# A transformer decoder on one core: the rotary swap of layer 2 by transfers, and a new order of two turns

## The chip, the cores and the metric

The kernel runs on one core of one Trainium2 chip. The metric is the device time of one execution in microseconds, as a median of several runs. The engines are TensorE (PE in the rows; PEld is its weight load), VectorE (DVE), ScalarE (ACT), GpSimd (POOL) and SyncE (SP), which here only issues transfers.

## The reference

128 sequences of 64 tokens with 128 features (`x`) go through four decoder layers. Each has an attention with 16 heads of 8 features, a cross attention to `ctx_1024` and a feed-forward part, each followed by a residual sum and a layer norm. What matters here is attention:

```
q, k, v = x @ wq + bq, x @ wk + bk, x @ wv          # per token; some layers without a bias
q, k    = rope(q), rope(k)                           # layers 0 and 2, and layer 3's cross attention
p       = softmax(q @ k.T / sqrt(8) + mask)          # per sequence and head, 64 x 64
x       = layernorm(x + (p @ v) @ wo + bo)
```

A rotation is `part * cos + swapped(part) * sin`. In layer 0 and layer 3 `swapped` exchanges neighbouring features. In layer 2 it exchanges the two halves of the 128 features: feature i with feature i + 64.

## The kernel before, in words

The 8192 tokens lie in 64 tiles of 128 rows in `X`, and all stages work on pairs of tiles (256 tokens, four sequences), so on 32 pairs. `attention(...)` builds one attention stage. It gives a generator per engine (`sync`, `gpsimd`, `tensor`, `scalar`, `vector`), whose `slot(T)` issues what the engine does in step T for several pairs at once; `all_pairs` runs the steps, those in the middle as a hardware loop of two pairs. The order within an engine is the order of the code, and semaphores (`made`, `parity_wait`) tie the engines together. Two stages can be run one behind the other, with the last four steps of the first interleaved with the first steps of the second: L1x with L1f, and L2a with L2x. L0a, L0x and L3x run alone. L1f and L2x share the memory, and so the tile names, of L1x and L2a.

What one pair passes through, with the step T in which it happens (T is the pair whose scores are made in this step):

- GpSimd copies its rows to `XS` (L498) in step T - 3. TensorE turns them into the bank `psF` (`fill_turn`, L584) in step T - 2, and ScalarE copies that to `XT` (L719; in L3x a copy of 512 columns, L717).
- In the same step TensorE projects `XT` to keys (`fill_projection`, L597) in `psF`, ScalarE copies them out, and then the queries follow in the same way. With rope (L0a, L2a, L3x) a second projection with swapped weights `ks`, `qs` gives the swapped part (L599), and ScalarE copies both parts with their biases to `RK` (`raw_parts`, L703 and L704). `psF` is one bank, so turn, keys, queries and values follow each other.
- GpSimd multiplies `RK` with the table of cosines and sines (`rope_product`, L404) and adds the two halves to the keys in `KT` (L524), and likewise to the queries in `QT` (L529). This stands at the end of its step, for pair T + 2. SyncE then sends the keys to `KB` in four transfers (L385), from where the scores use them.
- TensorE makes the scores in `psS` (L569), for L2a behind a fixed mask (L563). VectorE takes the maximum (L781) and subtracts it (L784), ScalarE takes the exponential (L756). In step T + 1 TensorE turns the probabilities (`turn_probs`, L617, four groups of four), ScalarE copies them (L697), TensorE multiplies them with the values (L683), and VectorE normalises to `ON` (L848).
- In step T + 2 TensorE turns `ON` (L630) into a half of the bank that the turned probabilities use too, ScalarE copies it to `OT` (L711), TensorE projects it (L672), and VectorE adds the residual rows (L816) and takes the statistics (L825, L836). The residual rows come with the bias added by GpSimd (`XR`, L482), except in L0x (`by_rows`), where TensorE adds the bias with a matmul (L670) and VectorE adds `X` itself.
- In step T + 3 GpSimd makes the root (L459, L461) and VectorE writes the normalised rows to `X` (L805).

In a step TensorE's order is: scores, turn of `ON` (L630), turn of the new rows (L584), first group of probabilities, key projection, two groups, query projection, last group, output projection, values times probabilities, value projection (`fill_v`, L609). ScalarE copies in the order `OT`, `XT`, first group, keys, two groups, queries, last group, then the exponential and the copy of the values to `VB` (L771). L0x gets its rows another way (`fill_rows`), without `fill_turn`; GpSimd rotates them as rows there (`rope_rows`).

## Time and profile before

| | us |
|---|---|
| median of 3 runs | 4016.08 (4015.06 to 4021.43) |
| the profiled execution | 4011.83 |
| its span, first to last instruction | 4010.0 |
| TensorE busy in it | 3481.2 |
| VectorE, ScalarE, GpSimd busy | 2993.7, 2291.8, 1885.8 |

The span and the busy times are of the one profiled execution; the median is of runs without a profile. Busy times are averages over stages with different limits, so the rows below are read stage by stage. In the execution L0a makes its scores from 27 to 309 us, L0x from 351 to 590, L1x and L1f from 1568 to 2067, L2a and L2x from 2409 to 2947, L3x from 3539 to 3857. The other parts of the span (routed experts, grouped attention, a recurrent block) are not touched.

### The profile page before, as it was taken

Reading aid. Unit: us, or ns where it says so; the run is one execution under the profiler, and the core shown is the slowest. Engines: PE = TensorE matmul, PEld = TensorE weight load, DVE = VectorE, ACT = ScalarE, POOL = GpSimd, SP = SyncE. Lnnn points to the kernel's source line nnn. Section 1 sums busy time; section 2 is a strip of 40 time slices with the busy share of each in tenths; the row PEclk is TensorE's granted clock in tenths of the full one; section 3 lists DMA queues with packets and bytes.
Section 4 is the critical chain, followed back from the end, with each engine's and each line's share of the span. In section 5 each row is a group of like instructions: output and inputs, shape, how many; then the busy total and the mean of one; then the engine's idle time right before and its main releaser. Section 6 shows DMA issues by size and latency. Waiting matters only on the chain. (4 is left out here: it accounts for less than half of the span.)

```text
span 4010.0 us, 127677 instructions
## 1 busy us (share of the span) xinstructions
PE 3481.2 (87%) x46840; PEld 2654.2 (66%) x46840; DVE 2993.7 (75%) x6186; ACT 2291.8 (57%) x3920; POOL 1885.8 (47%) x2970
## 2 busy tenths in 40 slices
PE   8996996797999998999987839999989688879985
PEld 6885775465777776878875627778854254457764
DVE  6986995155898886888863477888867588659975
ACT  5775771344444444778752447777754466556653
POOL 6887864655441111224545436652223355457754
PEclk9997995899999998999986969999989799989988
DMA  2002213697000000110005820001112000000001
GB/s 82 29 27 80 69 54 103 180 262 196 19 16 3 0 0 29 50 49 19 17 19 155 240 70 16 14 25 53 49 42 65 23 0 0 1 26 27 26 8 42
DMA packets 311910, 219.08 MB, mean 55 GB/s; under 512 B 52689, under 2 KB 290257, under 8 KB 311505
## 3 DMA queue, kind: packets, MB, share of 16 engines
q1 hardware_dynamic: 251824, 166.57, 14.3%
q0 software_dynamic: 12288, 25.19, 2.0%
q10 hardware_dynamic: 47520, 23.60, 2.0%
q8 instruction: 177, 2.90, 0.3%
q14 instruction: 101, 0.82, 0.1%
HBM read 131.27 MB, written 54.53 MB: 46 GB/s over the span
## 5 line engine op out<-in xcount | busy, mean ns | idle before, releaser
L781 DVE TENSOR_REDUCE L2a_mx<-L2a_psS 128x32 f32<-128x2048 f32 x64 | 146.7, 2292 | 75.8 <-PE L2a_psS L569 75.8
L781 DVE TENSOR_REDUCE L1x_mx<-L1x_psS 128x32 f32<-128x2048 f32 x64 | 146.7, 2292 | 74.5 <-PE L1x_psS L569 74.5
L2474 POOL TENSOR_TENSOR L1a_rs<-L1a_ag,eps 128x1 f32<-128x1 f32 x64 | 13.0, 204 | 397.8 <-DVE L1a_ag L2639 397.8
L1111 POOL DMA_INDIRECT L0f_sorted_x<-X,L0f_IDX x128 | 123.0, 961 | 93.8 <-DMA L0f_sorted_x<-X,L0f_IDX 35.6
L1530 DVE TENSOR_TENSOR L0f_G<-L0f_SG,L0f_psH 128x512 f32<-128x512 f32 x106 | 73.0, 689 | 120.1 <-ACT L0f_SG L1274 72.7
L459 POOL TENSOR_TENSOR L1x_rs<-L1x_mv,eps 128x2 f32<-128x2 f32 x64 | 12.5, 195 | 310.5 <-DVE L1x_mv L836 310.5
L784 DVE TENSOR_TENSOR L2a_PR<-L2a_psS,L2a_mx 128x2048 f32<-128x2048 f32 x64 | 146.7, 2292 | 7.3
L784 DVE TENSOR_TENSOR L1x_PR<-L1x_psS,L1x_mx 128x2048 f32<-128x2048 f32 x64 | 146.7, 2292 | 7.3 <-DVE L1x_mx L781 0.2
L697 ACT ACTIVATE L2a_PT<-L2a_psP 128x512 f32<-128x512 f32 x256 | 146.0, 598 | 2.9 <-PE L2a_psP L617 1.4
L697 ACT ACTIVATE L1x_PT<-L1x_psP 128x512 f32<-128x512 f32 x256 | 145.9, 595 | 3.0 <-PE L1x_psP L617 1.4
L617 PE MATMUL L1x_psP<-W,L1x_PR 128*128 128x128 f32 x1024 | 146.9, 277 | 0.2
L617 PE MATMUL L2a_psP<-W,L2a_PR 128*128 128x128 f32 x1024 | 145.7, 276 | 0.2
L756 ACT ACTIVATE L1x_PR<-L1x_PR 128x2048 f32<-128x2048 f32 x64 | 122.3, 1912 | 37.0 <-DVE L1x_PR L784 37.0
L2563 PE MATMUL L1a_psO<-rest_WO,L1a_OT 128*64 128x128 f32 x2048 | 125.9, 276 | 11.5 <-ACT L1a_OT L2588 7.4
L756 ACT ACTIVATE L2a_PR<-L2a_PR 128x2048 f32<-128x2048 f32 x64 | 122.6, 1915 | 18.5 <-DVE L2a_PR L784 18.5
L617 PEld LDWEIGHTS L1x_psP<-W,L1x_PR 128*128 128x128 f32 x1024 | 118.0, 142 | 20.7 <-ACT L1x_PT L697 13.9
L617 PEld LDWEIGHTS L2a_psP<-W,L2a_PR 128*128 128x128 f32 x1024 | 120.0, 142 | 17.6 <-ACT L2a_PT L697 7.9
L683 PE MATMUL L1x_psB<-VB,L1x_PT 128*64 128x18 f32 x4096 | 131.4, 212 | 0.0
L2497 PE MATMUL L1a_psF<-L1a_XT,rest_WQ 128*128 128x256 f32 x512 | 131.0, 390 | 0.5 <-DVE L1a_KT L2449 0.5
L2563 PEld LDWEIGHTS L1a_psO<-rest_WO,L1a_OT 128*64 128x64 f32 x2048 | 110.5, 137 | 31.4 <-ACT L1a_OT L2588 31.3
L683 PE MATMUL L2a_psB<-VB,L2a_PT 128*64 128x18 f32 x4096 | 131.2, 212 | 0.0
L683 PEld LDWEIGHTS L1x_psB<-VB,L1x_PT 128*64 128x64 f32 x4096 | 125.0, 138 | 7.8 <-issue 0.4
(624 smaller groups left out, 11625.1 us busy)
## 6 DMA issues: line engine op xcount, KB each, us to landing
L0f_WB<-in_w12a SPq DMA_DIRECT2D x53, 312.0 KB, 3.8
L0f_XB<-L0f_sorted_x SPq DMA_DIRECT2D x53, 256.0 KB, 4.0
L0f_sorted_y<-L0f_YB ACTq DMA_DIRECT2D x53, 256.0 KB, 3.8
L1m_WB<-in_w12b SPq DMA_DIRECT2D x37, 321.0 KB, 4.1
L1m_XB<-L1m_sorted_x SPq DMA_DIRECT2D x37, 256.0 KB, 4.0
L1m_sorted_y<-L1m_YB ACTq DMA_DIRECT2D x37, 256.0 KB, 4.4
L0x_VS<-in_ctx SPq DMA_DIRECT2D x64, 128.0 KB, 2.7
KB<-L1x_QK SPq DMA_DIRECT2D x256, 32.0 KB, 1.8
```

Source lines behind the costliest of these rows:

```text
L459: nc.gpsimd.tensor_tensor(rs[:, F.u, 0, :], mv[:, F.u, :, 1], eps[:, 0:2], ALU.add).then_inc(S["var_eps"].sem, 1)
L617: m = nc.tensor.transpose(psP[:, bank, n, :], PR[:, A.u, r, b:b + 2, :].rearrange("p h k -> p (h k)"), ident)
L683: m = nc.tensor.matmul(psB[64 * s:64 * s + 64, (j * HP + b) * VW:(j * HP + b + 1) * VW], PT[:, j, b, 64 * s:64 * s + 64], VB[:, A.u, 2 * j ...
L697: nc.scalar.activation(PT[:, j, 4 * hb:4 * hb + 4, :], psP[:, bank], ACT.Copy).then_inc(S["pt_a"].sem, 1)
L756: nc.scalar.activation(PR[:, T.u], PR[:, T.u], ACT.Exp, scale=scale).then_inc(S["probs"].sem, 1)
L781: nc.vector.tensor_reduce(mx[:, T.u, :], sc, AX, ALU.max).then_inc(S["maxed"].sem, 1)
L784: nc.vector.tensor_tensor(PR[:, T.u].rearrange("p r h k -> p (r h) k"), sc, mx[:, T.u, :].unsqueeze(2).to_broadcast([P, 2 * HEADS, SEQ]), ...
L1111: nc.gpsimd.indirect_dma_start(out=sorted_x[p][:, :], out_offset=bass.IndirectOffsetOnAxis(ap=IDX[:, k, t:t + 1], axis=0), in_=X[:, t, :], ...
L1530: nc.vector.tensor_tensor(G[0:f, J % 2, c, :], SG[0:f, c, :], up, ALU.mult).then_inc(S["g_ready"].sem, 1)
L2474: nc.gpsimd.tensor_tensor(rs[:, A.par, 0:1], ag[:, A.par, 1:2], eps[:, 0:1], ALU.add).then_inc(S["var_eps"].sem, 1)
L2497: m = nc.tensor.matmul(bank[:, 256 * j:256 * j + 256], WQ[:, 2 * k + j, :], XT[:, N.u, :], start=True, stop=True)
L2563: m = nc.tensor.matmul(psJ[64 * s:64 * s + 64, :], OT[:, s, c, :], WO[:, s, c, :], start=c == 0, stop=c == QC - 1, skip_group_check=True)
```

## The change

Three things change in `attention`.

- **The swap of layer 2 (L2a, `halves=True`).** The projections with swapped weights are gone, and so are their copies. ScalarE copies only the first part of keys and queries to `RK`, and SyncE makes the second part with two transfers per pair: partitions 64 to 127 to partitions 0 to 63, and the other way round, each of both keys and queries (64 partitions of two runs of 1 KB, 128 KB). They are issued behind the four key transfers of the pair before. `RK` gets two places. GpSimd's rotation moves from the end of its step, where it was for pair T + 2, to right behind the root, for pair T + 1, and waits for the transfers; the key transfers are for pair T + 1 as well.
- **The order.** TensorE turns the new rows (L584) ahead of `ON` (L630), and ScalarE copies `XT` ahead of `OT`. This holds for all stages but L0x.
- **The bias of L0x.** It is added by GpSimd to the residual rows, as in the other stages, and TensorE's matmul with it is gone.

The row writes (L805) stay as they were. On ScalarE a `pace` (one semaphore increment) stands ahead of the copies to `RK`.

```diff
@@ -251,13 +251,14 @@
-        def attention(L, q, k, v, o, qs=None, ks=None, bq=None, bqs=None, bk=None, bks=None, bo=None,
+        def attention(L, q, k, v, o, qs=None, ks=None, bq=None, bqs=None, bk=None, bks=None, bo=None, halves=False,
                       cq=0, ck=0, cross=False, norm=None, mask=None, ln_o=False, affine=None, keep=None, tally=False, arrive=False, tables=None, follows=None):
...
             by_rows = tables is not None
-            turned = ks is not None
+            turned = ks is not None or halves
+            ahead = 1 if halves else 2
             turn_c = cross and norm is not None and not by_rows
@@ -271,7 +272,7 @@
             RA = mem.sb("RA", [P, 2, 2, 2 * P]) if by_rows else None
-            RK = mem.sb("RK", [P, 2, 512]) if turned else None
+            RK = mem.sb("RK", [P, 2, 2, 512]) if turned else None
             QK = mem.sb("QK", [P, 2, 2, 2 * P])
@@ -313,8 +314,7 @@
             srcv = (CV if raw else CT) if cross else XT
-            bias_on_pe = by_rows
-            bias_row = rowx[:, 0, :] if ln_o else None if bias_on_pe else bo
+            bias_row = rowx[:, 0, :] if ln_o else bo
@@ -376,13 +376,22 @@
                         sp.dma_start(CV[:, K.u, :], io["ctxT"][:, bass.ds(K.p * 256, 256)]).then_inc(parity_sem("side_in", K), 16)
-                    if K.ok:
-                        made(sp, "k_roped" if turned else "o_k", K.p + 1)
+                    B = T + ahead if turned else K
+                    if B.ok:
+                        made(sp, "k_roped" if turned else "o_k", B.p + 1)
                         pace(sp, S)
-                        made(sp, "scores", K.p - 1)
+                        made(sp, "scores", B.p - 1)
                         for b in range(HQ):
-                            sp.dma_start(KB[b:P:HQ, K.u, b, :, :].rearrange("p s k -> p (s k)"), KT[b:P:HQ, K.u, :]).then_inc(parity_sem("keys_in", K), 16)
+                            sp.dma_start(KB[b:P:HQ, B.u, b, :, :].rearrange("p s k -> p (s k)"), KT[b:P:HQ, B.u, :]).then_inc(parity_sem("keys_in", B), 16)
+                    if halves and K.ok:
+                        made(sp, "o_k", K.p + 1)
+                        pace(sp, S)
+                        made(sp, "o_q", K.p + 1)
+                        for n in range(2):
+                            here, there = slice(64 * n, 64 * n + 64), slice(64 - 64 * n, 128 - 64 * n)
+                            sp.dma_start(RK[here, K.u, :, 256:512], RK[there, K.u, :, 0:256]).then_inc(parity_sem("stored", K), 16)
                     if mask is by_key and K.ok:
@@ -398,9 +407,13 @@
-            def rope_product(eng, n, tab):
-                parts = RK[:, n].rearrange("p (c s k) -> p c s k", c=2, s=4)
+            def kept(M):
+                return M.u if halves else 0
+            def rope_product(eng, M, n, tab):
+                parts = RK[:, kept(M), n].rearrange("p (c s k) -> p c s k", c=2, s=4)
                 return eng.tensor_tensor(parts, parts, rope[:, tab:tab + 2, :].unsqueeze(2).to_broadcast([P, 2, 4, SEQ]), ALU.mult)
@@ -442,6 +455,27 @@
+                def rotate(M):
+                    if turned and M.ok:
+                        if not products_on_dve:
+                            if halves:
+                                parity_wait(g, "stored", M, 32)
+                            else:
+                                made(g, "o_k", M.p + 1)
+                            rope_product(nc.gpsimd, M, 0, ck).then_inc(S["gates"].sem, 1)
+                        made(g, "gates", M.p + 1)
+                        parity_wait(g, "keys_in", M - 2, 16 * HQ)
+                        nc.gpsimd.tensor_tensor(KT[:, M.u], RK[:, kept(M), 0, 0:256], RK[:, kept(M), 0, 256:512], ALU.add).then_inc(S["k_roped"].sem, 1)
+                        if halves:
+                            parity_wait(g, "stored", M, 32)
+                        else:
+                            made(g, "o_q", M.p + 1)
+                        rope_product(nc.gpsimd, M, 1, cq).then_inc(S["gates_out"].sem, 1)
+                        made(g, "gates_out", M.p + 1)
+                        made(g, "scores", M.p - 1)
+                        nc.gpsimd.tensor_tensor(QT[:, M.u], RK[:, kept(M), 1, 0:256], RK[:, kept(M), 1, 256:512], ALU.add).then_inc(S["q_roped"].sem, 1)
@@ -465,6 +499,8 @@
                             nc.gpsimd.tensor_tensor(rows_of(F), RB[:, F.u], rs[:, F.u, 1, :].unsqueeze(2).to_broadcast([P, 2, D]), ALU.mult).then_inc(S["out_rows"].sem, 1)
+                    if halves:
+                        rotate(T + 1)
                     A = T - 2
@@ -513,20 +549,8 @@
                         mean_squares(N.p, CS[:, N.u], 0, MC[:, N.u, :], "stat_root", "means")
-                    M = T + 2
-                    if turned and M.ok:
...
+                    if not halves:
+                        rotate(T + 2)
                     Y = T - 4
@@ -622,6 +646,9 @@
                     yield
+                    if N.ok and not by_rows:
+                        fill_turn(N)
+                    yield
                     if H.ok:
@@ -629,9 +656,6 @@
                         m.then_inc(S["o_turned"].sem, 1)
-                    yield
-                    if N.ok and not by_rows:
-                        fill_turn(N)
                     yield
@@ -666,10 +690,8 @@
                             made(pe, "res", H.p)
-                        if bias_on_pe:
-                            nc.tensor.matmul(psJ, ident, bo.unsqueeze(1).to_broadcast([P, 2, D]), start=True, stop=False, skip_group_check=True)
                         for a in range(2):
-                            m = nc.tensor.matmul(psJ[:, a, :], OT[:, H.u, a * P:a * P + P], o, start=not bias_on_pe, stop=True, skip_group_check=bias_on_pe)
+                            m = nc.tensor.matmul(psJ[:, a, :], OT[:, H.u, a * P:a * P + P], o, start=True, stop=True)
                         m.then_inc(S["proj"].sem, 1)
@@ -696,20 +718,17 @@
-                def raw_parts(n, biases):
+                def raw_parts(N, n, biases):
+                    if halves:
+                        return nc.scalar.activation(RK[:, N.u, n, 0:256], psF[:, 0:256], ACT.Identity, bias=biases[0])
                     if biases[0] is None:
-                        return nc.scalar.activation(RK[:, n, :], psF[:, :], ACT.Copy)
-                    nc.scalar.activation(RK[:, n, 0:256], psF[:, 0:256], ACT.Identity, bias=biases[0])
-                    return nc.scalar.activation(RK[:, n, 256:512], psF[:, 256:512], ACT.Identity, bias=biases[1])
+                        return nc.scalar.activation(RK[:, 0, n, :], psF[:, :], ACT.Copy)
+                    nc.scalar.activation(RK[:, 0, n, 0:256], psF[:, 0:256], ACT.Identity, bias=biases[0])
+                    return nc.scalar.activation(RK[:, 0, n, 256:512], psF[:, 256:512], ACT.Identity, bias=biases[1])
...
                     A, N, H = T - 1, T + 2, T - 2 - e
-                    if H.ok:
-                        made(act, "o_turned", H.p + 1)
-                        made(act, "proj", H.p - 1)
-                        nc.scalar.activation(OT[:, H.u, :], flat(psOT), ACT.Copy).then_inc(S["ot"].sem, 1)
-                    yield
                     if N.ok and not by_rows:
@@ -717,6 +736,11 @@
                             nc.scalar.activation(XT[:, N.u, :], psF[:, 0:256], ACT.Copy).then_inc(S["o_tx"].sem, 1)
+                    yield
+                    if H.ok:
+                        made(act, "o_turned", H.p + 1)
+                        made(act, "proj", H.p - 1)
+                        nc.scalar.activation(OT[:, H.u, :], flat(psOT), ACT.Copy).then_inc(S["ot"].sem, 1)
                     yield
@@ -729,8 +753,9 @@
                         elif turned:
-                            made(act, "k_roped", N.p)
-                            raw_parts(0, (bk, bks)).then_inc(S["o_k"].sem, 1)
+                            made(act, "k_roped", N.p - 1 if halves else N.p)
+                            pace(act, S)
+                            raw_parts(N, 0, (bk, bks)).then_inc(S["o_k"].sem, 1)
                         else:
@@ -742,8 +767,9 @@
                         if turned:
-                            made(act, "q_roped", N.p)
-                            raw_parts(1, (bq, bqs)).then_inc(S["o_q"].sem, 1)
+                            made(act, "q_roped", N.p - 1 if halves else N.p)
+                            pace(act, S)
+                            raw_parts(N, 1, (bq, bqs)).then_inc(S["o_q"].sem, 1)
                         else:
...
@@ -2670,8 +2697,8 @@
-        turning = attention("L2a", Wm("L2q"), Wm("L2k"), Wm("L2v"), Wm("L2o"), qs=Wm("L2qs"), ks=Wm("L2ks"), bq=C("L2bq"), bqs=C("L2bqs"),
-                  bk=C("L2bk"), bks=C("L2bks"), bo=rowb[:, 2, :], cq=2, ck=2, mask=static)
+        turning = attention("L2a", Wm("L2q"), Wm("L2k"), Wm("L2v"), Wm("L2o"), halves=True, bq=C("L2bq"), 
+                  bk=C("L2bk"), bo=rowb[:, 2, :], cq=2, ck=2, mask=static)
         run(turning, attention("L2x", Wm("L2xq"), Wm("L2xk"), Wm("L2xv"), Wm("L2xo"), bq=C("L2xbq"), bk=C("L2xbk"), bo=rowb[:, 3, :], cross=True, follows=turning))
```

## Rows read from the trace of the kernel before

**Rows 1.** Line L781, one stretch per stage: duration ns; first to last start, us.

```profile
L781 DVE TENSOR_REDUCE L0x_mx<-L0x_psS x27: 2280/2291/2292, 368.9 to 567.8; 128x32 f32<-128x2048 f32 x27
...
L781 DVE TENSOR_REDUCE L1x_mx<-L1x_psS x26: 2291/2292/2292, 1601.0 to 1802.1; 128x32 f32<-128x2048 f32 x26
...
L781 DVE TENSOR_REDUCE L2a_mx<-L2a_psS x27: 2291/2292/2293, 2446.6 to 2687.9; 128x32 f32<-128x2048 f32 x27
...
L781 DVE TENSOR_REDUCE L2a_mx<-L2a_psS x28: 2291/2292/2293, 2720.1 to 2931.7; 128x32 f32<-128x2048 f32 x28
...
L781 DVE TENSOR_REDUCE L3x_mx<-L3x_psS x27: 2280/2292/2294, 3571.5 to 3838.4; 128x32 f32<-128x2048 f32 x27
```

**Rows 2.** Stretches: us; busy us (count) of PE, PEld, DVE, ACT, POOL; clock; DMA.

```profile
100.00:190.00 90.00, 88.17 (x1596) 73.73 (x1596) 81.60 (x140) 63.73 (x111) 76.60 (x161) 1.00 0.09 29
430.00:540.00 110.00, 98.91 (x1749) 83.69 (x1747) 106.85 (x156) 82.39 (x130) 96.89 (x172) 1.00 0.23 69
2480.00:2640.00 160.00, 154.44 (x2779) 127.49 (x2777) 140.41 (x191) 118.54 (x222) 102.16 (x138) 1.00 0.04 14
3620.00:3800.00 180.00, 170.90 (x2605) 133.58 (x2603) 169.33 (x318) 123.79 (x226) 133.65 (x212) 1.00 0.08 26
```

**Rows 3.** Timeline, TensorE, a pair of L2a: start, length in us, instruction [idle].

```profile
2548.38 0.44 PE L630 MATMUL L2a_psP<-W,L2a_ON 128*128 128x128 f32 x2
2548.66 0.38 PE L584 MATMUL L2a_psF<-W,L2a_XS 128*128 128x128 f32 x2
2548.88 0.60 PE L617 MATMUL L2a_psP<-W,L2a_PR 128*128 128x128 f32 x4
2549.65 0.70 PE L597 MATMUL L2a_psF<-L2a_XT,W 128*128 128x256 f32 x2 [0.17 <-ACT L2a_XT L719]
2550.18 0.59 PE L599 MATMUL L2a_psF<-L2a_XT,W 128*128 128x256 f32 x2
2550.61 1.04 PE L617 MATMUL L2a_psP<-W,L2a_PR 128*128 128x128 f32 x8
2551.79 0.48 PE L597 MATMUL L2a_psF<-L2a_XT,W 128*128 128x256 f32 x1
...
2556.35 0.64 PE L563 MATMUL L2a_psS<-causal,pick 32*64 32x512 bf16 x16
```

**Rows 4.** Timeline of GpSimd and SyncE in the same pair of L2a.

```profile
2551.81 1.28 POOL L404 TENSOR_TENSOR L2a_RK<-L2a_RK,rope 128x512 f32<-128x512 f32 x1 [2.33 <-ACT L2a_RK L704]
2553.17 0.73 POOL L524 TENSOR_TENSOR L2a_QK<-L2a_RK 128x256 f32<-128x256 f32 x1
...
2554.06 2.39 SPq L385 DMA_DIRECT2D KB<-L2a_QK  x4
```

**Rows 5.** Transfers of the run: count, KB each, us from issue to landing.

```profile
L0x_VS<-in_ctx SPq DMA_DIRECT2D x64, 128.0 KB, 2.7
...
KB<-L2a_QK SPq DMA_DIRECT2D x256, 32.0 KB, 1.8
...
L2a_CR<-in_ctxT SPq DMA_DIRECT2D x32, 128.0 KB, 2.1
```

**Rows 6.** Groups by line, L2a, last L2x: count | busy us, mean ns.

```profile
L805 DVE TENSOR_SCALAR X<-L2a_RB,L2a_mv,L2a_rs 128x128 f32 x29 | 30.0, 1072 | 0.0
...
L482 POOL TENSOR_TENSOR L2a_XR<-X,rowb 128x256 f32<-128x256 f32 x14 | 10.4, 743 | 0.0
...
L805 DVE TENSOR_SCALAR X<-L2a_RB,L2a_mv,L2a_rs 128x128 f32 x26 | 7.7, 340 | 0.0
```

**Rows 7.** Timeline of ScalarE and TensorE at a step's start in L2x.

```profile
2813.16 0.78 ACT L771 ACTIVATE VB<-L2a_psF 64x256 f32<-64x256 f32 x2
...
2814.10 0.44 PE L630 MATMUL L2a_psP<-W,L2a_ON 128*128 128x128 f32 x2
```

**Rows 8.** Waits of TensorE, 120 us of L3x: us in total, times, longest.

```profile
PE L3x_psF L597 <- ACT L3x_CX L717: 3.5, 12, 0.3
```

**Rows 9.** Waits of GpSimd in 90 us of L0x.

```profile
POOL L0x_rs L459 <- DVE L0x_mv L836: 10.3, 12, 0.9
```

14 lines of the change are left out of this document (2 added, 12 removed).

## The prediction

> **What bounds the kernel now.** The change touches seven attention stages that have one loop body. Each handles 32 pairs of tiles, so the first thing to read is the time per pair. [rows 1] gives it, as the distance from the first to the last reduction of a stretch over the number of steps between them. L0x takes (567.8 - 368.9) / 26 = 7.65 us, L1x 201.1 / 25 = 8.04, L2a 241.3 / 26 = 9.28, L2x 211.6 / 27 = 7.84 and L3x 266.9 / 26 = 10.27. L0a is not shown; L1f, which follows L1x as L2x follows L2a, has the work of L2x.
>
> Next come the busy times of such stretches [rows 2]. In L2a TensorE is busy for 154.4 of 160 us and VectorE for 140.4, so TensorE is the bound. In L0x VectorE is busy for 106.9 of 110, TensorE for 98.9 and GpSimd for 96.9: VectorE is the bound, with GpSimd not far behind. L0a (TensorE 88.2 of 90) and L3x (170.9 of 180) are bound by TensorE too, though in L3x VectorE (169.3) is almost level. TensorE's granted clock is 1.00 in all four, the 2.4 GHz level; with TensorE as full as this after the change I see no reason for it to fall.
>
> Then one pair of L2a on TensorE [rows 3]. Matmuls overlap, so a group's cost is the time from its start to the next group's start; where nothing is waited for, that is its modelled length less 0.17 (L597: 0.70 long, L599 starts 0.53 later). A swapped twin, L599, costs 0.43 (2550.18 to 2550.61), and there are two of them per pair. The four transposes at 2548.88 should cost 0.60 - 0.17 = 0.43, but the key projection starts 0.77 after them: TensorE stands for 0.33 us until ScalarE has copied XT. The eight at 2550.61 should cost 0.87, but the query projection starts 1.18 after them: it stands for 0.3 us, now because ScalarE must copy the keys and their swapped twin out of the bank first. These two stalls and the two twins are what the change reaches.
>
> **L2a, part by part.** The swapped halves of keys and queries no longer come from a second projection, so two L599 groups of 0.43 go: -0.86 per pair. The key copy on ScalarE is one activation in place of two, and is done some 0.4 us earlier; the 0.3 us stall before the query projection goes with it, since the eight transposes cover one copy of half a microsecond. The third part is the order. Now the input rows are turned second (L584, 0.28 after L630) and copied after the turned output. Ahead of it, the copy starts 0.28 earlier and the key projection with it; about 0.06 of the stall stays, so -0.27. Together 9.28 - 0.86 - 0.30 - 0.27 = 7.85. A second way: L2x has the same work per pair without swapped halves and without the fixed mask. It takes 7.84; the mask group costs 0.64 - 0.17 = 0.47 (L563), and the new order takes 0.27 off: 8.04. TensorE's bound lies between the two, 7.85 to 8.04.
>
> What takes the projection's place is a ring that did not exist before: GpSimd multiplies and adds the keys, SyncE sends the rotated keys, and behind these on the same queue sends the two swap transfers of the next pair, for which GpSimd waits. The key product starts at 2551.81 and the addition ends at 2553.90, which is 2.1; the four key transfers are issued until 2556.45 [rows 4], another 2.55. About 0.2 for SyncE's waits and 0.5 for the issue of the first swap (four key transfers take 2.39 to issue, 0.6 each) bring the sum to 5.4, and 0.1 for the semaphores to 5.5. Then the landing of the second swap, X. The trace has no transfer of 128 KB between partitions, so I bound X by its neighbours [rows 5]: 1.8 for 32 KB from one place of SBUF to another, 2.1 for 128 KB onto all partitions, 2.7 for 128 KB onto 64 partitions, two of which are issued back to back just as here. I take 2.5, near the last, which has the same form but twice the packets. The ring then needs 5.5 + 2.5 = 8.0 us per pair (7.3 to 8.2 over the bounds), as much as TensorE. I take 8.0 for L2a, 1.28 less than now, and for 32 pairs **-41 us** (bounds -34 and -46). The start of the stage, where the first keys wait for a transfer but the twins are gone from the chain, I put at nothing, within 3 us.
>
> What hides the rest: GpSimd does the rotation directly behind the small root, so while VectorE does its two passes over the scores (2.29 each). So far it falls together with L805, two of which take 1.07 us each in L2a and 0.34 in L2x, where GpSimd has little to do [rows 6]. After the change the two products and additions (4.2), GpSimd's bias addition (0.74) and the row copy end some 5.3 us after the start, about when L805 begins (two passes, 4.9), so VectorE gains up to 2 x 0.73 us per pair, which nobody waits for, as VectorE is not the bound. Behind the waiting product on GpSimd stand the bias addition, which VectorE needs in the same step, and the copy of the rows, a whole step ahead; if the swap is late by more than about half a microsecond, the addition is late too. The keys have landed 2.1 + 2.55 - 0.6 + 1.8 = 5.9 us after the product starts, and the scores want them 2556.35 - 2548.38 - 1.43 = 6.5 after the first turn, so 0.5 us of delay is covered there as well. The two paces on ScalarE are a few hundredths each, in idle time.
>
> **The order alone, in the other stages.** In L0a, L1x, L1f, L2x and L3x only the turn of the input rows moves. The stall before the key projection is the same 0.33, and the most that can be gained is 0.27 a pair. But the turn then has to wait for the copy of the values out of the same PSUM bank, right after the scores. In L2x that copy ends at 2813.94 and TensorE reaches this place at 2814.10 [rows 7]: with a semaphore's some 0.06 only 0.1 of the 0.27 can be had, since the copy is behind the exponential and this behind VectorE's passes. I take 0.07 for L2x and for L1f: -4 together. L1x has a mask group between and so more room; I take 0.22, -7. In L3x the stall is 3.5 us in 12 pairs in the view of waits [rows 8], but four transposes have to end first, which leaves about 0.18 of gain: -5, if VectorE follows, which has 10.27 x (1 - 0.94) = 0.6 us of idle time in a pair. In L0a GpSimd is busy for 76.6 of 90 us and its chain of small sums has gaps of its own, so I take half of 0.27: -4. Bounds for these five stages: 0 and -30, together.
>
> **L0x: the bias.** TensorE loses one matmul of 256 columns (0.53, as L597), which does not count, because VectorE is the bound. GpSimd gets an addition of 0.74 (743 ns in L2a [rows 6], 0.70 start to start). It waits for VectorE's statistics for 10.3 us in 12 pairs, 0.86 each [rows 9], so the addition fits, with 0.1 to 0.2 left. Two sides: GpSimd now is busy at all times when L805 runs, which may cost VectorE up to 0.3 a pair; or L805 falls behind another of GpSimd's instructions and is done sooner, and then GpSimd's own chain is the bound, 7.65 - 0.86 + 0.70 and about 0.1 for a semaphore, 7.6. I take 0, bounds -3 and +10.
>
> **Sum.** -41 - 4 - 7 - 5 - 4 + 0 = -61 on the profiled execution's 4011.8 us, so 3951. That execution is 4.3 us under the median of 4016.1, which gives **3955**.
>
> **Rivals.** (1) *The ring of transfers is the bound in L2a.* TensorE then waits for keys in each pair, and the engine shares fall. For it: the swaps are queued behind four key transfers, and transfers onto 64 partitions are the slower ones [rows 5]. At X from 2.8 to 3.6 a pair takes 8.3 to 9.1: L2a gives 31 to 6 us, and the time is 3965 to 3990. The Trainium skill, "DMA: Bandwidth & Descriptors", section "Rules for kernel authors", says of two transfers to disjoint partition halves that they serialize and that one 128-partition transfer should be used instead. The rows agree as far as they go, 2.7 against 2.1; by that rule alone X would be 2.7 to 2.8 and L2a 8.2 to 8.3, which is where this rival begins.
>
> (2) *The order brings nothing*, because the copy of the values or GpSimd is always the later one: the other stages give 0 and L2a 1.28 - 0.27 per pair, so -32 and 3984. Against it: TensorE waits for the copy of the rows in every pair (12 times in 12 pairs in [rows 8]), and for nothing else that is as long.
>
> (3) *GpSimd becomes the bound in L0x and L0a*: +10 and 0 in place of 0 and -4, so 3969. For it: GpSimd has 0.1 to 0.2 us left in L0x. "SBUF — State Buffer", section "Who interferes with whom", in the Trainium skill, says that VectorE in its two-port mode and GpSimd exclude each other for whole instructions; L805 at 1.07 us beside a busy GpSimd agrees, and by that rule L0x would sit on this side.
>
> (4) *Slower than before*: the swaps land so late that L2a takes longer than now by more than the other stages win. That needs (20 + 0) / 32 = 0.6 us over 9.28, a ring of 9.9 and X of 4.4 us, more than one and a half times the longest 128 KB row. At X = 5.5 a pair takes 11.0: +55 - 20, so 4050. Only if the swap transfers break into far more pieces than the code suggests.
>
> **Chances.** The forecast 0.52 (own range 3940 to 3965), rival 1 0.22, rival 2 0.10, rival 3 0.10, rival 4 0.06. The low end takes every bound on its good side: 46 in L2a and 3 at its start, 0.27 x 32 = 9 each in L1x and L0a, 6 in L3x, 6 in L1f and L2x, 3 in L0x, 82 in all, so 3934. The high end, 3988, takes in rivals 2 and 3 and most of rival 1. Faster by over 0.2% (8 us, about what a measurement of this kernel can tell from no change): 0.92; within it 0.03; slower 0.05.
>
> **What would show it.** L599 gone and L2a at 7.9 to 8.1 per pair; the wait of the key projection for XT gone or under 0.1 us in L2a and L1x; L805 in L2a well under 1.07 us; in L2x and L1f nearly the old pace, with TensorE's idle time now in front of the turn; GpSimd's wait for the statistics in L0x shrunk from 0.86 to about 0.1 and 7.65 kept. The forecast is wrong if GpSimd's key product in L2a waits for the swap transfer in each pair and the scores for keys (rival 1), if the reductions of L0x are more than 7.8 apart (rival 3), or if the other stages keep their periods to 0.02 (rival 2).

## The result, and the profile after

The changed kernel takes 3952.99 us (median, 3946.19 to 3967.05), the kernel before 4015.57 us beside it. The ratio is 0.9847, with a 95% interval of 0.9818 to 0.9876. The predicted 3955 us is 2 us away. The profiled execution took 3952.28 us with a span of 3950.5, which is 59.5 less than before.

A sum that comes out right can hide terms that did not, so the first thing to read is the length of each stage. The reductions stand in line L807 of the changed kernel and in L781 of the one before. The columns are the count, the duration (least, median, most, in ns) and the first and last start in us. L1x and L2a have 64 reductions, since L1f and L2x share their tile names. After:

```profile
L807 DVE TENSOR_REDUCE L1x_mx<-L1x_psS x64: 2290/2291/2292, 1559.9 to 2040.2; 128x32 f32<-128x2048 f32 x64
L807 DVE TENSOR_REDUCE L2a_mx<-L2a_psS x64: 2290/2291/2294, 2384.5 to 2886.4; 128x32 f32<-128x2048 f32 x64
L807 DVE TENSOR_REDUCE L0a_mx<-L0a_psS x32: 2290/2291/2293, 29.4 to 302.0; 128x32 f32<-128x2048 f32 x32
L807 DVE TENSOR_REDUCE L0x_mx<-L0x_psS x32: 2278/2290/2292, 347.5 to 584.0; 128x32 f32<-128x2048 f32 x32
L807 DVE TENSOR_REDUCE L3x_mx<-L3x_psS x32: 2278/2290/2292, 3484.0 to 3796.2; 128x32 f32<-128x2048 f32 x32
```

Before, from the same view of the whole run:

```profile
L781 DVE TENSOR_REDUCE L1x_mx<-L1x_psS x64: 2291/2292/2294, 1570.7 to 2066.4; 128x32 f32<-128x2048 f32 x64
L781 DVE TENSOR_REDUCE L2a_mx<-L2a_psS x64: 2291/2292/2293, 2411.0 to 2946.7; 128x32 f32<-128x2048 f32 x64
L781 DVE TENSOR_REDUCE L0a_mx<-L0a_psS x32: 2291/2292/2294, 29.9 to 308.1; 128x32 f32<-128x2048 f32 x32
L781 DVE TENSOR_REDUCE L0x_mx<-L0x_psS x32: 2280/2291/2292, 353.0 to 589.7; 128x32 f32<-128x2048 f32 x32
L781 DVE TENSOR_REDUCE L3x_mx<-L3x_psS x32: 2280/2292/2294, 3542.7 to 3856.2; 128x32 f32<-128x2048 f32 x32
```

Last start less first start gives the lengths. The two double stages are split at their 33rd reduction (2704.7 and 2651.7 us in layer 2, 1825.6 and 1806.2 in layer 1).

| stage | before, us | after, us | difference | predicted |
|---|---|---|---|---|
| L0a | 278.2 | 272.6 | -5.6 | -4 |
| L0x | 236.7 | 236.5 | -0.2 | 0 |
| L1x | 254.9 | 246.3 | -8.6 | -7 |
| L1f and L2x | 482.8 | 468.7 | -14.1 | -4 |
| L2a | 293.7 | 267.2 | -26.5 | -41 |
| L3x | 313.5 | 312.2 | -1.3 | -5 |
| outside the stages | | | -3.2 | 0 |

So L2a brought 14 us less than forecast, and L1f and L2x brought 10 us more. The parts outside the stages were not changed. From the last reduction of L1f to the first of L2a there are 344.3 us here, and 334.5 and 347.8 in two of the kernels below, so -3.2 is no more than one execution differs from another.

The stretches that answer to [rows 2] are the same in time, so they lie a little later in the stages. The columns are the stretch, its length, the busy us (count) of PE, PEld, DVE, ACT and POOL, the clock and the DMA's share:

```profile
100.00:190.00 90.00, 89.89 (x1641) 75.36 (x1626) 82.22 (x142) 65.22 (x114) 77.11 (x161) 1.00 0.09 29
430.00:540.00 110.00, 90.73 (x1714) 76.43 (x1708) 107.42 (x160) 80.56 (x127) 104.96 (x185) 1.00 0.22 67
2480.00:2640.00 160.00, 154.73 (x2989) 129.10 (x2987) 140.30 (x213) 119.58 (x217) 116.34 (x158) 1.00 0.19 48
3620.00:3800.00 180.00, 173.81 (x2695) 135.39 (x2695) 173.51 (x324) 125.10 (x227) 130.63 (x206) 1.00 0.07 23
```

The granted clock stays at 1.00, the 2.4 GHz level. In L0a TensorE now has nothing but work. In L0x GpSimd's busy time rose from 96.9 to 105.0 of 110 us. In L2a TensorE is not quite full, and the view of waits says why. Its columns are the waiting instruction, what ended the wait, the total in us, the times and the longest. In 110 us of L2a, from 2490:

```profile
POOL L2a_RK L417 <- DMA L2a_RK<-L2a_RK: 4.9, 13, 0.4
...
PE L2a_psS L587 <- issue: 1.3, 7, 0.2
PE L2a_psS L587 <- DMA KB<-L2a_QK: 1.0, 5, 0.2
```

GpSimd's key product waits for the swap transfer in each of 13 pairs, and TensorE stands for some 0.2 us ahead of the scores. This is the sign that the prediction gave for its first rival. One turn of the ring can be followed in the timeline (start, length, instruction, idle time ahead of it):

```profile
2544.90 1.27 POOL L417 TENSOR_TENSOR L2a_RK<-L2a_RK,rope 128x512 f32<-128x512 f32 x1 [0.41 <-DMA L2a_RK<-L2a_RK]
...
2546.34 0.73 POOL L469 TENSOR_TENSOR L2a_QK<-L2a_RK 128x256 f32<-128x256 f32 x1 [0.17 <-POOL L2a_RK L417]
...
2547.22 2.42 SPq L386 DMA_DIRECT2D KB<-L2a_QK  x4
...
2549.90 1.33 SPq L394 DMA_DIRECT2D L2a_RK<-L2a_RK  x2
...
2553.02 1.28 POOL L417 TENSOR_TENSOR L2a_RK<-L2a_RK,rope 128x512 f32<-128x512 f32 x1 [0.33 <-DMA L2a_RK<-L2a_RK]
```

Product and addition take 2.17, the semaphore to SyncE 0.15, the issue of the keys 2.42, SyncE's waits 0.26 and the issue of the first swap 0.69. By the transfer's own record the second swap, issued at 2550.59, lands at 2552.95, so X is 2.36. With 0.07 for the semaphore that is 8.12 us from product to product, as the two product rows say.

### The profile page after: what moved, and what is told of

Same layout as the page of the kernel before. It is cut to its first block and busy times, and to the rows that moved or that the text cites. A ratio compares the mean times of both kernels' runs of the same rounds, so it can differ in the third digit from the quotient of the medians.

```text
span 3950.5 us, 127503 instructions
## 1 busy us (share of the span) xinstructions
PE 3432.6 (87%) x46648; PEld 2618.2 (66%) x46648; DVE 2964.8 (75%) x6186; ACT 2252.1 (57%) x3856; POOL 1900.4 (48%) x3002
## 5 line engine op out<-in xcount | busy, mean ns | idle before, releaser
L807 DVE TENSOR_REDUCE L2a_mx<-L2a_psS 128x32 f32<-128x2048 f32 x64 | 146.6, 2291 | 78.1 <-PE L2a_psS L593 78.1
L807 DVE TENSOR_REDUCE L1x_mx<-L1x_psS 128x32 f32<-128x2048 f32 x64 | 146.6, 2291 | 69.4 <-PE L1x_psS L593 69.4
L705 PEld LDWEIGHTS L2a_psB<-VB,L2a_PT 128*64 128x64 f32 x4096 | 124.6, 138 | 7.9 <-issue 0.4
```

The costliest lines, as they stand in the source:

```text
L705: m = nc.tensor.matmul(psB[64 * s:64 * s + 64, (j * HP + b) * VW:(j * HP + b + 1) * VW], PT[:, j, b, 64 * s:64 * s + 64], VB[:, A.u, 2 * j ...
L807: nc.vector.tensor_reduce(mx[:, T.u, :], sc, AX, ALU.max).then_inc(S["maxed"].sem, 1)
```

## The experiments

Each experiment is read by stage, because the untouched parts differ by more than many of the effects. "Steady L2a" is the mean of the 14 steps after the first 12 of the stage, from the reductions' starts. Before it is 9.32 us (2520.7 to 2651.1), after 8.15 (2487.6 to 2601.8); the starts are rounded here, the means are not. The other stages are read over some 18 steps in their middle.

### The parts of the change, one at a time

The first kernel is the changed one without the new order and with the bias of L0x on TensorE. The second is the kernel before with the new order alone:

```diff
                     if T.ok:
                         scores(T)
                     yield
+                    if N.ok and not by_rows:
+                        fill_turn(N)
+                    yield
                     if H.ok:
...
-                    if N.ok and not by_rows:
-                        fill_turn(N)
-                    yield
```

(with ScalarE's copy of `OT` behind that of `XT` likewise). The third is the kernel before with the bias alone:

```diff
-            bias_on_pe = by_rows
-            bias_row = rowx[:, 0, :] if ln_o else None if bias_on_pe else bo
+            bias_row = rowx[:, 0, :] if ln_o else bo
...
-                        if bias_on_pe:
-                            nc.tensor.matmul(psJ, ident, bo.unsqueeze(1).to_broadcast([P, 2, D]), start=True, stop=False, skip_group_check=True)
```

> The kernel before with the swap by transfers and the moved rotation in L2a alone; the order of the turns and the bias of L0x as before. If the swap's gain is its own, L2a goes from 9.28 us per pair to about 8.2 (the ring of product, addition, four key transfers and two swaps took 8.12 in the trace after the change), and since the ring and not TensorE is the limit there, the old order costs L2a nothing: the whole kernel gains 31 to 36 us. Rival: TensorE is the limit in L2a and the order is part of its gain; then L2a is at 8.4 or more here, as the stall of 0.27 comes back, and the gain is 25 us. All other stages keep their old periods: L1x 8.04, L2x 7.84, L3x 10.27.

> The kernel before with the new order of the two turns and copies alone. If the stages other than L2a gained by the order, L1x goes to 7.75 us per pair, L1f and L2x to 7.6, L0a to 8.8, L3x to 10.13, as in the trace after the change, and L2a, which has its twins still, from 9.28 to 9.0: 20 + 9 = about 30 us together, more than the 20 + 9 - 0 that I forecast for L1f and L2x at 0.07 each by some 9. Rival: the gain in L1f and L2x comes in part from the earlier end of L2a or another phase against it; then they stay at 7.7 or above here and the kernel gains under 20 us.

> The kernel before with the bias of L0x on GpSimd alone. Forecast: VectorE is the limit of L0x and GpSimd has room for the addition, so 0 us, between -3 and +4; the period of L0x stays at 7.65 to 7.8 and GpSimd's wait for the statistics falls from 0.86 us per pair to about 0.1. Rival: GpSimd becomes the limit, 7.9 or more per pair and +8 us; or TensorE's lost matmul was on the path, 7.2 and -14 us.

| kernel | median, us | ratio to before (95%) | steady L2a | L0a, L0x, L1x, L2x per pair |
|---|---|---|---|---|
| before | 4015.56 | 1 | 9.32 | 9.03, 7.73, 8.07, 7.84 |
| swap alone | 3991.85 | 0.9947 (0.9930 to 0.9964) | 8.26 | 9.12, 7.72, 8.08, 7.84 |
| order alone | 3980.63 | 0.9922 (0.9899 to 0.9944) | 9.00 | 9.07 (a mean of two paces, see below), 7.72, 7.76, 7.61 |
| bias alone | 4005.36 | 0.9978 (0.9966 to 0.9990) | 9.32 | 9.02, 7.46, 8.08, 7.86 |
| all three | 3952.99 | 0.9847 (0.9818 to 0.9876) | 8.15 | 8.81, 7.79, 7.77, 7.60 |

The swap alone takes 1.05 us off a pair of L2a, and its 24 us are short of the 31 to 36 expected: it reads 8.26, between the forecast and the rival. The order alone takes 0.32 off where TensorE is the bound, in L2a and L1x alike. Behind the swap it takes only 0.11 off L2a, the sign of a second limit. The bias alone, expected to be nothing, made L0x faster; it is taken up below. Alone the three bring 24, 35 and 10 us, 69 together, and all three 63: they do not simply add, because of that second limit and because L0x and L0a have more than one pace, as will be seen.

### Is the ring the limit of L2a?

Two kernels bear on it. In one the first swap transfer goes out on ScalarE's queue, which shortens the ring and changes no transfer:

```diff
-                        for n in range(2):
+                        for n in range(1, 2):
                             here, there = ...
                             sp.dma_start(RK[here, K.u, :, 256:512], RK[there, K.u, :, 0:256]).then_inc(parity_sem("stored", K), 16)
...
+                    if halves and N.ok:
+                        made(act, "o_q", N.p + 1)
+                        act.dma_start(RK[0:64, N.u, :, 256:512], RK[64:128, N.u, :, 0:256]).then_inc(parity_sem("stored", N), 16)
```

> The changed kernel with one of the two swap transfers issued by ScalarE's queue, behind its last copy of the turned probabilities, in place of SyncE's. Ring theory: SyncE has 0.69 us less to issue between the keys of one pair and the landing of the swap of the next, so the ring falls from 8.12 to 7.4 and TensorE is the limit at 7.95 per pair; GpSimd's product no longer waits for the transfer, TensorE not for keys, and stalls from single late transfers get shorter: -6 to -12 us against the changed kernel, 3941 to 3947. Rival: TensorE is the limit at 8.15 already: no change, or some us more, as the issue of 0.64 us delays ScalarE's exponential.

In the other a third transfer of the same form goes into a scratch tile, ahead of the two:

```diff
+                        sp.dma_start(RZ[0:64, K.u, :, :], RK[64:128, K.u, :, 0:256]).then_inc(parity_sem("stored", K), 16)
                         for n in range(2):
...
-                                parity_wait(g, "stored", M, 32)
+                                parity_wait(g, "stored", M, 48)
```

> The changed kernel with a third transfer of the same form (64 partitions, 128 KB) in front of the two swap transfers of each pair of L2a; it writes into a scratch tile, and GpSimd waits for all three. Theory (the ring of GpSimd, four key transfers and two swap transfers sets L2a's pace): the ring gets one more issue on SyncE's queue, 0.65 us, and if the three share the DMA engines the landing grows a little too: a pair of L2a takes 8.19 + 0.65 = 8.85 us (up to 9.1), and the kernel gets 20 us slower than the changed one (20 to 28), about 3973 to 3981. Rival (TensorE sets the pace at 8.1 to 8.2 and the ring only keeps step with it): up to 0.1 us per pair, under 5 us in all.

The reductions of the 15 steady pairs, first with two queues, then with a third transfer:

```profile
L810 DVE TENSOR_REDUCE L2a_mx<-L2a_psS x15: 2291/2292/2293, 2474.9 to 2588.1; 128x32 f32<-128x2048 f32 x15
```

```profile
L809 DVE TENSOR_REDUCE L2a_mx<-L2a_psS x15: 2290/2290/2292, 2494.5 to 2618.2; 128x32 f32<-128x2048 f32 x15
```

With two queues a pair takes 113.2 / 14 = 8.09, and neither GpSimd's wait for the swap nor TensorE's for the keys is left in the view of waits of 2480 to 2600: that is TensorE's own pace, with 118.3 of 120 us busy. With the third transfer it takes 123.7 / 14 = 8.84, 0.69 more than the changed kernel, one issue on SyncE's queue; the kernel takes 3972.25 us (ratio 0.9895, 0.9873 to 0.9918), 19 more. In 100 us of it, from 2500, both waits have grown:

```profile
POOL L2a_RK L419 <- DMA L2a_RK<-L2a_RK: 11.7, 11, 1.2
...
PE L2a_psS L589 <- DMA KB<-L2a_QK: 7.2, 9, 1.0
```

So the ring sets L2a's pace, but by a hair: 8.15 against TensorE's 8.09. Two more executions with two queues, further down, have 8.09 again. The kernel with two queues takes 3937.27 us (ratio 0.9813, 0.9790 to 0.9837), 16 less than the changed kernel's 3953 (11 less than in its second run, below) and less than either expectation gave. The whole time says little of L2a, though. Of the 14 us between the two profiled executions some 3 are L0x and 3 L0a; 7.5 are L2a, and of these only 14 x 0.07 = 1 us falls in the steady part.

The rest of the 7.5 us is at the edges of the stage. The first 12 steps of L2a take 109.7 us before, 103.1 after and 98.1 with two queues. At the steady difference of 1.16 the change should have taken 14 us off them, and took 6.6; with two queues they lose almost nothing against 12 x 8.09. This holds beyond one execution, though by less: the first 12 steps take 100.2, 100.3 and 101.7 in three more executions with the changed kernel's code in L2a, and 97.1 and 97.3 in two more with two queues. The DMA view of the changed kernel shows what is different there. First 2410 to 2462, where steps of 9.3 to 10.1 us stand, then 2500 to 2552, a steady stretch (queue: packets, MB, share; issues: count, KB, median us to landing):

```profile
q1 hardware_dynamic: 2878, 2.36, 17.6%
q8 instruction: 6, 0.10, 0.9%
q14 instruction: 2, 0.02, 0.1%
...
L2a_RK<-L2a_RK SPq DMA_DIRECT2D x12, 128.0 KB, 3.0
```

```profile
q1 hardware_dynamic: 3185, 2.61, 19.3%
...
L2a_RK<-L2a_RK SPq DMA_DIRECT2D x14, 128.0 KB, 2.4
```

Where the queues that bring in instructions are active, a swap lands after 3.0 us in place of 2.4 (median), and the product waits up to 1.7 us in place of 0.4. Single issues on SyncE are longer there too: two of a key transfer took 1.76 and 1.51 us and one of a swap 1.62, in place of 0.6. So the four key transfers of one long step take 3.58 us to issue, where they take 2.42 in the turn above:

```profile
2420.17 3.58 SPq L386 DMA_DIRECT2D KB<-L2a_QK  x4
```

Such packets and such issues are there in the other kernels as well. In the kernel before five issues in the first 12 steps took 0.9 to 1.6 us; its second step is long (10.34), but from the third on none is over 9.38. With two queues two issues took 1.4, and the longest of the first 12 steps is 8.96. That the lack of slack makes late transfers cost time is shown by the kernel with two queues; that it is those packets which delay the issues and the transfers is a coincidence in time, and was not tested by itself.

### The place of the rotation in GpSimd's step

```diff
-                    if halves:
-                        rotate(T + 1)
                     A = T - 2
...
-                    if not halves:
-                        rotate(T + 2)
+                    rotate(T + (1 if halves else 2))
```

> The changed kernel with the rotation of L2a at the end of GpSimd's step, behind its addition of the bias and its copy of the rows, in place of directly behind the small root. Theory: there is a second ring beside that of the transfers, over two pairs: scores, VectorE's statistics, GpSimd's root, key product and addition, key transfers, scores. It takes some 15.7 us per two pairs now and gets 1.2 longer: L2a 8.35 to 8.5 per pair, 5 to 10 us more than the changed kernel; VectorE's row write takes about 1 us per tile again in place of 0.42 to 0.71. Rival (the place in GpSimd's step only decides what the row write falls together with, the transfers' ring alone sets the pace): L2a stays at 8.2 within 0.05, no difference in time over 3 us.

The row writes (L831 after, L828 in this kernel; count, busy us, mean ns of one, idle ahead) in 110 us of L2a, first after (where it was 1072 ns before, [rows 6]), then with the late rotation:

```profile
L831 DVE TENSOR_SCALAR X<-L2a_RB,L2a_mv,L2a_rs 128x128 f32 x28 | 14.3, 551 | 0.0
```

```profile
L828 DVE TENSOR_SCALAR X<-L2a_RB,L2a_mv,L2a_rs 128x128 f32 x28 | 8.3, 340 | 0.0
```

Both expectations missed something. The pair takes 8.27 us in place of 8.15, less than the 8.35 to 8.5 of the theory and more than the rival's 0.05. A second ring fits, if its 15.7 us contained the product's own wait for the swap, some 0.4 us, which the late rotation uses up: (15.7 - 0.4 + 1.2) / 2 = 8.25. This sum was made after the result. It agrees that GpSimd waits for the swap no more, and that TensorE waits for the keys for 4.0 us in 13 pairs in place of 1.0. And the row write got shorter, not longer: in its new place the rotation has VectorE's two passes beside it. The kernel takes 3943.62 us (ratio 0.9828, 0.9805 to 0.9851); that it is below the changed kernel is no gain of L2a. In the profiled executions L2a takes 1.5 us more, L0x at 7.47 us per pair takes 6.7 less, and the untouched part between L1f and L2a 7.8 less.

### What limits L1f and L2x

The second half of the value copy is left out in L1f and L2x:

```diff
-                        for a in range(2):
+                        for a in range(2 if follows is None else 1):
```

> The changed kernel with the second of ScalarE's two value copies (0.39 us) left out in L1f and L2x, so half of the values there are not the right ones. Theory of the prediction (the copy of the values out of the bank limits the turn of the input rows in these stages): L1f and L2x go from 7.58 and 7.60 us per pair to 7.48 to 7.52, 5 to 7 us less than the changed kernel in all. Rival (TensorE alone sets their pace, the order has given its whole gain there): both stay within 0.02, no difference in time over 2 us.

L1f went from 7.58 to 7.53 and L2x from 7.60 to 7.53, between the two expectations: the value copy does hold the turn back, but by 0.05 to 0.07 us per pair and not by 0.2. The lengths of L1f and L2x fall by 3.5 us together. (The kernel takes 3940.43 us, 13 less than the changed one; most of the rest is L0x at 7.47 and the edges of L0a and L2a.) What remains is TensorE, which is busy for 149.7 of 150 us there.

### Two paces in L0x, and one in L0a

The bias alone had made L0x faster, 7.46 in place of 7.73 us, though the changed kernel, with the same code there, has 7.79. The changed kernel was therefore run once more:

> The changed kernel once more, unaltered, to see whether the pace of L0x (7.79 us per pair in the profiled execution of the changed kernel, 7.46 in two other kernels with the same code in L0x) goes with the execution or with the kernel. Theory (two ways for VectorE's row write and GpSimd's instructions to fall together, chosen anew in each execution by how the stage starts): L0x takes 7.46 or 7.79 here, nothing between; the other stages stay within 0.05 of the first look. Rival (the rest of the kernel decides): 7.79 again, within 0.02, and the same irregular pairs in L2a.

It has 7.80 again, and takes 3947.85 us (ratio 0.9834, 0.9806 to 0.9862). The waits and the row writes (430 to 530 us) of the changed kernel:

```profile
POOL L0x_rs L493 <- DVE L0x_mv L862: 3.3, 13, 0.3
...
L831 DVE TENSOR_SCALAR X<-L0x_RB,L0x_mv,L0x_rs 128x128 f32 x26 | 20.6, 833 | 0.0
```

In the bias alone there is no wait of GpSimd for the statistics in that stretch, and its row writes (L802) are shorter:

```profile
L802 DVE TENSOR_SCALAR X<-L0x_RB,L0x_mv,L0x_rs 128x128 f32 x28 | 17.8, 675 | 0.0
```

In the quick pace GpSimd never stands, and its own chain, 7.46, is the bound. In the slow one VectorE's two row writes together take 0.3 us longer, VectorE is the bound, and GpSimd waits for its statistics. That it is GpSimd's instructions which hold the row writes is read from how they fall together, not tested by itself. Two kernels put the bias addition ahead of the root, so that GpSimd has work there; the second has the two queues in L2a too:

```diff
+                    J = T - 2 - e
+                    if by_rows and J.ok and bias_row is not None:
+                        made(g, "res", J.p - 1)
+                        nc.gpsimd.tensor_tensor(XR[:, J.u], rows_of(J), bias_row.unsqueeze(1).to_broadcast([P, 2, D]), ALU.add).then_inc(S["xres"].sem, 1)
                     F = T - 3 - e
...
-                    J = T - 2 - e
-                    if J.ok and bias_row is not None:
+                    if not by_rows and J.ok and bias_row is not None:
```

> The changed kernel, with GpSimd's addition of the bias in L0x put ahead of its small root in place of behind it. In the two profiled executions of the changed kernel with 7.79 us per pair in L0x, GpSimd stands for 0.3 us in each pair in front of the small root, which needs VectorE's statistics; in those with 7.46 it never stands there. Theory (the slower pace is this wait, fed by VectorE's row write, which is held by GpSimd's instructions): with 0.73 us of work put in front of the root the statistics are always there in time, GpSimd never stands and L0x takes 7.46 +- 0.04 per pair; other stages as before; about 3943 to 3947. Rival (VectorE's row write is held by whatever GpSimd does then, and VectorE sets the pace): 7.6 to 7.9 per pair and GpSimd still stands somewhere, 3948 to 3955.

> The kernel with the first swap transfer of L2a issued from ScalarE's queue, and with the bias addition of L0x ahead of the root. Theory: L2a at TensorE's 8.1 per pair, L0x at 7.46; 3933 to 3941, the same as the kernel with the two queues alone was in an execution that had 7.46 in L0x. Rival (the two gains meet, or L0x falls into the slower pace): 3943 or more.

The first has 7.46 and takes 3939.97 us (ratio 0.9825, 0.9804 to 0.9847), the second has 7.69 and takes 3940.27 us (0.9815, 0.9794 to 0.9836). The same code in L0x gave both paces, so the place of the bias does not settle it, and that theory falls. Last, the second of them was run once more:

> The last kernel (two queues, and the bias addition of L0x ahead of the root) once more, unaltered. L0x took 7.69 us per pair in its first look, and 7.46 in another kernel with the same code in L0x. Theory (each execution chooses its pace anew): 7.46 here is as likely as 7.69, and 7.46 would show it. Rival (the kernel as a whole decides): 7.69 again, within 0.02.

The reductions of L0x from 420 us on, in the first execution and in the second:

```profile
L814 DVE TENSOR_REDUCE L0x_mx<-L0x_psS x13: 2280/2291/2294, 420.5 to 512.8; 128x32 f32<-128x2048 f32 x13
```

```profile
L814 DVE TENSOR_REDUCE L0x_mx<-L0x_psS x13: 2280/2290/2292, 423.0 to 512.6; 128x32 f32<-128x2048 f32 x13
```

92.3 / 12 = 7.69 and 89.6 / 12 = 7.47 us, with one and the same kernel (3938.34 us the second time, ratio 0.9818, 0.9801 to 0.9834). So the kernel alone does not fix the pace. Of ten profiled executions with the bias on GpSimd seven had 7.46 or 7.47 and three 7.69 to 7.80. What chooses is open. The two executions were on different chips, so this pair does not part the chip from the execution. The chip alone does not settle it: on the chip with the changed kernel's 7.80, three kernels with the same code in L0x had 7.46 or 7.47. Nor is it excluded that the rest of the kernel has a say, since the changed kernel had the slow pace both times.

L0a showed the like. The order alone had 9.07 us per pair there, all three parts 8.81. One kernel adds the pace on ScalarE to the order:

```diff
                             made(act, "k_roped", N.p)
+                            pace(act, S)
...
                             made(act, "q_roped", N.p)
+                            pace(act, S)
```

> The new order alone, with the pace instruction that the change puts on ScalarE ahead of its copies to RK, in L0a, L2a and L3x. It looks for what L0a's 8.81 us per pair in the changed kernel need beside the order: the order alone had 9.07, where VectorE's row write waited 1.0 us in each pair for GpSimd's root. Theory (the two paces shift ScalarE by some hundredths and with it which of VectorE's instructions GpSimd's small ones meet): L0a 8.81, 6 to 8 us less than the order alone, about 3973. Rival (the pace is nothing, the layout of RK or the execution decides): L0a 9.07 within 0.03, the time of the order alone, 3981 within 3.

L0a takes 8.81 and the kernel 3977.01 us (ratio 0.9912, 0.9893 to 0.9931), as the theory had it, though the ranges of the two kernels' times overlap and 3.6 us are no more than their spread. In the order alone VectorE's row write waits for GpSimd's root in every pair of 150 to 250 us:

```profile
DVE X L805 <- POOL L0a_rs L461: 10.3, 11, 1.0
```

In its timeline the root's first addition starts 0.05 us into VectorE's key product and takes 0.69 us:

```profile
204.62 0.68 DVE L404 TENSOR_TENSOR L0a_RK<-L0a_RK,rope 128x512 f32<-128x512 f32 x1
204.67 0.69 POOL L459 TENSOR_TENSOR L0a_rs<-L0a_mv,eps 128x2 f32<-128x2 f32 x1
```

In the timeline of the changed kernel it comes first and takes 0.19:

```profile
202.03 0.19 POOL L493 TENSOR_TENSOR L0a_rs<-L0a_mv,eps 128x2 f32<-128x2 f32 x1
...
202.52 0.68 DVE L417 TENSOR_TENSOR L0a_RK<-L0a_RK,rope 128x512 f32<-128x512 f32 x1
```

The wait is gone with the paces, but it does not take them to be rid of it. The 9.07 of the order alone is a mean over a change in mid-stage: from 49.3 to 136.0 us its pairs take 8.67 each, from 144.9 to 282.6 us 9.18. The root's first addition (L459) tells the two parts apart, here over 60 to 135 and 150 to 290 us (duration least, median, most, in ns):

```profile
L459 POOL TENSOR_TENSOR L0a_rs<-L0a_mv,eps x8: 194/194/197, 65.9 to 131.2; 128x2 f32<-128x2 f32 x8
```

```profile
L459 POOL TENSOR_TENSOR L0a_rs<-L0a_mv,eps x16: 582/636/685, 149.5 to 287.2; 128x2 f32<-128x2 f32 x16
```

So the order alone brings its gain in L0a too, as long as the root stays ahead of the key product, and one execution can leave that pace with no change in the code. That the paces hold L0a in the quicker one is possible and not shown.

## Why the prediction was right in the sum, and where its steps were not

**L2a, the twins and the stalls: right.** L599 is gone, and so are both stalls. In the pair that answers to [rows 3] each projection follows its transposes without a gap, 0.43 and 0.89 us after their starts:

```profile
2544.92 0.60 PE L641 MATMUL L2a_psP<-W,L2a_PR 128*128 128x128 f32 x4
...
2545.35 0.68 PE L621 MATMUL L2a_psF<-L2a_XT,W 128*128 128x256 f32 x2
...
2545.87 1.04 PE L641 MATMUL L2a_psP<-W,L2a_PR 128*128 128x128 f32 x8
...
2546.76 0.70 PE L621 MATMUL L2a_psF<-L2a_XT,W 128*128 128x256 f32 x2
```

TensorE's own pace, measured with the ring out of the way, is 8.09, 0.05 over the 7.85 to 8.04 given.

**L2a, the ring: the mechanism of rival 1 at almost the forecast's price.** Forecast 5.5 + 2.5 = 8.0, measured 8.12 in the pair above. X is 2.36 and not 2.5, between the 128 KB rows of [rows 5]. The terms that were too small are the issue of the first swap (0.69, not 0.5, though the key transfers beside it took 0.60 each) and SyncE's waits (0.26, not 0.2). A steady pair gained 1.16 us and not 1.28, which costs 32 x 0.12 = 4 us. The tie forecast between ring and TensorE was 8.15 against 8.09, so the ring is the bound, and the third transfer shows it.

**L2a, the edges: the step that failed.** I put the start of the stage at nothing, within 3 us. Of the 14 us that L2a fell short, 7.4 lie in its first 12 steps and 3.3 in the steps after the steady ones (53.6 before, 49.9 after for six, where 7 were due). The step left out that a ring without slack turns each late transfer into a late pair. The kernel with two queues, whose edges lose next to nothing, shows that it is this; with 100.2 to 101.7 us in three other executions, up to 3 us of the 7.4 belong to this one.

**The Trainium skill's rule.** "DMA: Bandwidth & Descriptors", section "Rules for kernel authors", says that two transfers to disjoint partition halves serialize. By that rule alone X would have been 2.7 to 2.8. Here the second landed 0.67 us after the first (2552.28 and 2552.95), their issues were 0.69 apart, and the second landed 2.36 after its own issue, the first 2.38: no added time is to be seen. One 128-partition transfer in place of the two was not tried.

**L1f and L2x: right mechanism, wrong size.** I gave them 0.07 us per pair and they brought 0.22 and 0.24. I had read that the value copy ends 0.16 us ahead of the turn [rows 7], and that it stands behind the exponential and VectorE's passes, so that only 0.1 was to be had. But the copy waits for two things, and in the kernel before the other one came last. The view of the timeline a pair earlier says it:

```profile
2805.41 0.78 ACT L771 ACTIVATE VB<-L2a_psF 64x256 f32<-64x256 f32 x2 [0.17 <-PE L2a_psF L609]
```

The copy was waiting for TensorE's value matmuls, which come earlier with all of TensorE's work. In the pair of [rows 7] it started 1.96 us after the exponential did (2811.20 to 2813.16); after the change 1.82 (2800.56 to 2802.38). Over 19 and 22 pairs of L2x the means are 2.02 and 1.84, and before the change the copy starts 0.13 us after the end of the value matmuls. The other 0.07 is that VectorE starts 0.10 us after the turn's start and not 0.17, on average over the same pairs. The limit itself is real: half the value copy less gave another 0.05 to 0.07.

**L1x: right**, -8.6 for -7. The stall is wholly gone, 0.30 per pair, where 0.06 was to stay. **L0a** got 0.22 per pair, where I had taken half of 0.27; the order alone kept its gain there for a third of the stage only. **L3x** won 0.15 per pair, from 10.32 to 10.17, as forecast (0.18), but the step that starts the stage is 2.8 us longer in this execution.

**L0x: right by luck.** -0.2 for 0. The prediction had both sides, VectorE held longer by GpSimd's instructions, and GpSimd's own chain as the bound. It started from 7.65 us per pair, a mean with the stage's shorter first steps (the middle ones take 7.73), and gave the second side 7.6; it is 7.46, worth 7 us, and the more frequent of the two. Three of ten executions show the slower side, and the two of the changed kernel are among them. The bound of -3 was too narrow: the bias alone brought 7 us in L0x. GpSimd's wait for the statistics shrank to 0.25 us per pair, where 0.1 was the sign given.

**The sum.** The misses cancel: +14.5 us in L2a, -10.1 in L1f and L2x, +0.3 in the other stages together (-1.6 in L0a and L1x each, -0.2 in L0x, +3.7 in L3x) and -3.2 outside the stages, so -59.5 in place of -61. Rival 2 falls with the order alone, which brings 35 us. Rival 3 falls with L0x no slower than before; its sign, reductions more than 7.8 us apart, was just missed, at 7.79 and 7.80. Rival 4 falls with X at 2.36.

## What to carry to other kernels

Before a transfer is put in place of computation, write its ring down term by term, issue by issue; if it comes out within a few tenths of the engine's own pace, give it slack by a second queue, because a late transfer at a stage's edges can then cost a late pair. Where an instruction waits for two things, look at neighbouring pairs to see which one came last: only the one that does not move with the change is a limit. And where two engines hold each other's instructions up, read more than one execution of the same kernel, stage by stage, before a few microseconds are put down to an edit.

## What the runs showed of the hardware that was not expected

- A stage of two coupled engines has two paces with one and the same kernel: 7.47 and 7.69 us per pair in L0x, each held from the ninth step to the last few, and in L0a with the order alone 8.67 and 9.18, with a change between them in mid-stage.
- A row write of 128 x 128 takes 0.34 us on VectorE with GpSimd at rest (late rotation, L2a) and 0.68 to 0.83 on average beside a busy GpSimd; the small root's first addition on GpSimd takes 0.19 us alone and 0.69 when VectorE's key product has started just before it. This agrees with "SBUF — State Buffer", section "Who interferes with whom", in the Trainium skill, which has the two engines exclude each other for whole instructions.
- An SBUF-to-SBUF transfer of 128 KB onto 64 partitions takes 0.64 us to issue and lands after 2.4 us; in a stretch with packets of the instruction queues it landed after 3.0 (medians), and single issues took 1.5 to 1.8 us.
